# Layer statistics of two pairs on ScalarE, one scale on GpSimd, one block of zero matmuls out, and a new order of steps

## What is computed

```python
qf = jnp.fft.fft(q, axis=2)
kf = jnp.fft.fft(k, axis=2)
corr = jnp.fft.ifft(qf * jnp.conj(kf), axis=2).real
w, idx = jax.lax.top_k(corr.transpose(0, 1, 3, 2), topk)      # topk = 8
w = jax.nn.softmax(w, axis=-1)
out = sum over i of w_i * v[min(pos + idx_i, L - 1)]
...
x = x + jnp.tanh(g_xattn[0]) * xattn(_layernorm(x), ctx, ctx)
x = x + jnp.tanh(g_ffn[0]) * ffn(_layernorm(x), W_gate, W_up, W_down)   # (silu(gate) * up) @ W_down
```

## Time and profile before

| | us |
|---|---|
| median of 3 runs (213.5 to 214.62) | 214.24 |
| span of the profiled execution | 212.1 |
| TensorE busy in it | 203.6 |
| VectorE | 135.7 |
| ScalarE | 131.4 |
| GpSimd | 122.4 |

### The profile page before, as it was taken

How to read it: one execution, slowest core, us unless ns; L and a number is a source line. 1 busy time by engine, 2 the same in 40 slices (tenths; PEclk the granted TensorE clock), 3 DMA queues, 4 the chain that set the end, 5 groups by cost and what they waited for, 6 DMA issues and landing times.

```text
span 212.1 us, 6601 instructions
## 1 busy us (share of the span) xinstructions
PE 203.6 (96%) x2700; PEld 147.8 (70%) x2700; DVE 135.7 (64%) x408; ACT 131.4 (62%) x207; POOL 122.4 (58%) x151
## 2 busy tenths in 40 slices
PE   7889799999999999999999999999999999999993
PEld 2344369855398866795689665896598669859992
DVE  2499978977987884689478933898454426412411
ACT  2581776789897989697947894986335713502220
POOL 1200658588598977589848596797724734610430
PEclk9999999999999999999999999999999999999999
DMA  6999986420222201002011211120213300211001
GB/s 154 338 416 434 389 297 137 106 44 12 49 35 47 25 3 38 14 3 51 0 28 30 49 28 25 53 53 2 71 31 66 134 3 0 77 25 53 5 0 51
DMA packets 20734, 17.89 MB, mean 84 GB/s; under 512 B 16096, under 2 KB 16992, under 8 KB 20320
## 3 DMA queue, kind: packets, MB, share of 16 engines
q1 hardware_dynamic: 20704, 17.47, 27.5%
HBM read 10.65 MB, written 2.10 MB: 60 GB/s over the span
## 4 chain that ended last, share of the span: by engine, by line
PE 89%; DVE 5%; ACT 1%; DMA 1%; issue 1%; POOL 1%; DVEq 0%; POOLq 0%
PE psum L937 48%; PE psum L1121 23%; PE psum L920 6%; PE psum L1071 3%; PE psum L928 2%; PE psum L1056 2%; DMA x_sb<-x 1%; PE psum L1048 1%; PE psum L1014 1%; DVE top L792 1%; DVE probs L814 1%; DVE raw_stats L759 1%; PE psum L1016 1%; PE psum L1015 1%; DVE prod L782 1%
## 5 line engine op out<-in xcount | busy, mean ns | idle before, releaser
L937 PE MATMUL psum<-xt_hi,wu 128*128 128x128 f16 (+1 forms) x504 | 54.0, 213 | 0.0
L937 PE MATMUL psum<-xt_lo,wu 128*128 128x128 f16 (+1 forms) x504 | 54.0, 213 | 0.0
L937 PE MATMUL psum<-xt_hi,wg 128*128 128x128 f16 (+1 forms) x504 | 54.0, 213 | 0.0
L937 PE MATMUL psum<-xt_lo,wg 128*128 128x128 f16 (+1 forms) x504 | 53.9, 213 | 0.0
L632 POOL TENSOR_TENSOR hid_lo<-hid,hid_hi 128x512 f16<-128x512 f32 (+2 forms) x32 | 33.6, 1055 | 28.8 <-ACT hid_hi L750 28.7
L937 PEld LDWEIGHTS psum<-xt_hi,wg 128*128 128x128 f16 x504 | 44.8, 98 | 5.6 <-issue 5.0
L937 PEld LDWEIGHTS psum<-xt_hi,wu 128*128 128x128 f16 x504 | 45.0, 98 | 3.2 <-issue 2.4
L937 PEld LDWEIGHTS psum<-xt_lo,wu 128*128 128x128 f16 x504 | 45.1, 98 | 0.7
L937 PEld LDWEIGHTS psum<-xt_lo,wg 128*128 128x128 f16 x504 | 45.0, 98 | 0.6
L1121 PE MATMUL psum<-wd,hid_hi 128*128 128x512 f16 (+1 forms) x126 | 43.3, 356 | 0.0
L1121 PE MATMUL psum<-wd,hid_lo 128*128 128x512 f16 (+1 forms) x126 | 43.3, 355 | 0.0
(11 more groups left out here) (95 smaller groups left out, 340.9 us busy)
## 6 DMA issues: line engine op xcount, KB each, us to landing
wg<-w_gate SPq DMA_DIRECT2D x1, 1792.0 KB, 8.9
wu<-w_up SPq DMA_DIRECT2D x1, 1792.0 KB, 12.8
wd<-w_down SPq DMA_DIRECT2D x1, 1792.0 KB, 16.9
out<-x_sb SPq DMA_DIRECT2D x7, 256.0 KB, 2.3
...
ctx_sb<-ctx SPq DMA_DIRECT2D x1, 1024.0 KB, 18.6
...
```

What stands on the lines that cost most here:

```text
L937: last = nc.tensor.matmul(psum[:, bank, a * n:(a + 1) * n], w[:, k, m * P:(m + 1) * P], xt[:, e, k, tok], start=(k == 0 and part == 0), st ...
```

## The change

First statistics of pairs 1 and 2. The step `stats1` is gone for them. Instead ScalarE copies `x` with its accumulator on (`xsum`, the sum over 512 columns), GpSimd makes the negative mean (`negmean`), ScalarE squares `x` minus the mean with its accumulator on (`xsq`), and `rstd1` on GpSimd works from that sum of squares. `normed` takes the copies, which nobody reads. The scale of the second batch of pair 0 (`scale:0.1`) goes from VectorE to GpSimd. The second block of zero matmuls is left out, the first stays.

Further: the token buffers `xt_hi` and `xt_lo` are four instead of two; every step of `down` signals its end, and `h_hi` waits for the step that frees its part; `w_whole` lies in `v_turned`, so that the turn of pair 2 waits for `wspec:0.1`; the second half of the last store is issued from ScalarE's queue. The functions for groups of pairs do nothing new here, since every group has one pair. And the table `ORDER` is a new one as a whole.

```diff
-vcopy:1 mask:0 max:0.1 kcopy:1.1 scale:0 sub8:0.1 wt:0 stats1:2 exp8:0.1 w_hi:0 match:0.1 gates:0 wspec:0
+mask:0 kcopy:1 turn:1.3 scale:0 max:0.1 q_norm:1 wt:0 sub:0.1 w_hi:0 match:0.1 kcopy:1.1 wspec:0 sub8:0.1 xsum:2
...
-ON_VECTOR = (("scale", 0, 0), ("scale", 0, 1),)
+ON_VECTOR = (("scale", 0, 0),)
+SUMMED = (1, 2)
...
-    w_whole = sb("w_whole", [P, 2, D])
+    w_whole = v_turned[:, 0, :, :]
...
-                        if p >= 2:
-                            sp.wait_ge(up_done, STEPS * (p - 1))
+                        if p >= 4:
+                            sp.wait_ge(up_done, tokens_used(p))
...
+                if step == "negmean":
+                    pool.wait_ge(summed, SUMMED.index(p) + 1)
+                    nc.gpsimd.tensor_scalar(minus_mean[:, e:e + 1], x_sum[:, e:e + 1], -1 / D, None,
+                                            ALU.mult).then_inc(mean_ready, 1)
+                if step == "rstd1" and p in SUMMED:
+                    pool.wait_ge(squared, SUMMED.index(p) + 1)
+                    nc.gpsimd.tensor_scalar(var_eps[:, e:e + 1], square_sum[:, e:e + 1], 1 / D, EPS, ALU.mult,
+                                            ALU.add).then_inc(eps1, 1)
...
+                if step == "scale" and p == 0 and mine:
+                    to = twice(n)
+                    pool.wait_ge(inv_ready, nth("total", p, n))
+                    pool.wait_ge(masked, nth("mask", p, n))
+                    nc.gpsimd.tensor_tensor(to, lag_cols(expo, p, n).unsqueeze(2).broadcast_to(to.shape),
...
+                if step == "xsum":
+                    act.wait_ge(x_loaded[load_of(p)], 16)
+                    if p >= 2 and p - 2 in WHOLE_SPECTRA:
+                        act.wait_ge(q_spectra, p - 1)
+                    nc.scalar.activation(normed[:, e, :], x_sb[:, p, :], ACT.Copy,
+                                         accum_out=x_sum[:, e:e + 1]).then_inc(summed, 1)
+                if step == "xsq":
+                    act.wait_ge(mean_ready, SUMMED.index(p) + 1)
+                    nc.scalar.activation(normed[:, e, :], x_sb[:, p, :], ACT.Square, bias=minus_mean[:, e:e + 1],
+                                         accum_out=square_sum[:, e:e + 1]).then_inc(squared, 1)
...
-                        act.wait_ge(down_done, p - 1)
+                        act.wait_ge(down_step, hidden_free(p, n))
...
+                if step == "store_half":
+                    act.wait_ge(out_ready, PAIRS + 1)
+                    nc.scalar.dma_start(outv[:, p:p + 1, halves(p)[1]], x_sb[:, p:p + 1, halves(p)[1]])\
+                      .then_inc(half_stored, 16)
```

290 lines of the change are left out of this document (174 added, 116 removed).

## The result

The changed kernel took 215.97 us in the median of six executions (214.19 to 217.05), the kernel before 214.09 (213.5 to 214.62, six executions). The ratio is 1.0083, with a 95% interval of 1.0051 to 1.0115. The forecast was 213.3, and its range ended at 214.8.

What follows compares the result with a forecast made beforehand. TensorE, full from 28 to 208 us, was taken as the bound, leaving only prologue and end to gain. 0.8 us at the front plus 0.1 at the end, off 214.24, gave 213.3 us, range 212.4 to 214.8.

Steps and rivals of the forecast that it cites:

- The front: Prologue up to gate:0: w_hi:0 at 14.2, mix_prod:0 at 16.0, max:1 near 20.8, gate:0 earlier by 0.8 us.
- the order of `max:0.1` and `scale:0`: VectorE in the prologue: scale:0 ahead of max:0.1 takes 0.53 us off the path, 0.10 given back.
- the place of `scale:0.1`: VectorE from mix_prod:0 to max:1: scale:0.1 goes out, four small steps come in, net gain 0.18 us.
- the sum: Whole kernel: 0.8 us at the front plus 0.1 at the end, 0.9 us off the time.
- pair 2's statistics: Prologue: leaving VectorE gives nothing; on ScalarE two activations between 15.7 and 17.6 us, through before anyone waits.
- The accumulator: ScalarE, two more activations per pair: each at least 0.54 us, at most 0.80 plus 0.2 for reading the sum.
- The rival that put ScalarE late: Prologue: accumulators cost 0.6 us more than taken up to w_hi:0, giving 214.0 us; chance 0.17.
- `scale:0.1` on GpSimd: Prologue: 1.04 us on GpSimd, from near 19.3 to 20.4, hidden by 0.3 us behind lags:1.
- The end: Last stores: the second issued from ScalarE's queue instead of SyncE's, gain 0.1 us, bounds 0 and 0.2.
- The turns: SyncE's queue: eight DMAs of pairs 1 and 2 moved ahead of pair 1's first weight transposes, no cost.
- The clock: TensorE in the prologue, second zero block out: clock falls, 2.8 us more, 216.1 us; chance 0.10.
- New order opens holes: Full stretch, 28 to 208 us: holes of 0.69 us, one gives 214.0, three 215.4; chance 0.10.

Runs made afterwards that it cites:

- e9: Kernel before with max:0.1 behind scale:0 on VectorE, scale:0.1 on GpSimd behind lags:1 and the second store split off: 213.72 us beside 213.79, ratio 1.0002.
- e10: Changed kernel's order up to gate:0 with five zero matmuls, gates:0, k_hi:3, k_lo:3 and turns at their old places, old order behind: 213.71 us beside 213.79.
- e11: Kernel before with the statistics of pairs 1 and 2 on ScalarE's accumulator, each where its step stood, second store split off: 216.95 us beside 213.79, ratio 1.0104.
- e12: Kernel before with SyncE's turns of pairs 1 and 2 moved ahead, nothing else: 217.50 us beside 213.79, ratio 1.0132.
- e1: Changed kernel with five zero matmuls put back ahead of wt:0: 215.51 us beside 213.78, ratio 1.0064.
- e5: e1 with SyncE's turns of pairs 1 and 2 put back behind w_t:1 and w_t:1.1: 214.52 us beside 213.90, ratio 1.0023.
- e17: The changed kernel as it is, timed again beside the kernel before: 215.86 us beside 213.94, ratio 1.0083.
- e18: Changed kernel with only the turns put back behind w_t:1 and w_t:1.1, second zero block still out: 215.82 us beside 213.94, ratio 1.0029.
- e2: Kernel before without its second block of zero matmuls, nothing else changed: 215.26 us beside 213.78, ratio 1.0075.
- e6: Kernel before up to gate:0, the changed kernel's order from there on, turns where they stood: 214.91 us beside 213.90, ratio 1.0045.
- e13: e10 with a third block of four zero matmuls ahead of wspec:0.1: 213.41 us beside 213.91, ratio 0.9989.
- e16: e13 with the one 1 MB load of ctx moved to just ahead of w_t:2: 213.89 us beside 213.94, ratio 0.9984.

## Why the prediction was wrong, step by step

**The front: right.** `w_hi:0` was forecast at 14.2 and stands at 14.02, `mix_prod:0` at 16.0 and stands at 15.84, `max:1` at 20.8 and stands at 20.71. The gain at `gate:0` is 0.9 us where 0.8 was said. How it was shared out was less right: e9 shows that the order of `max:0.1` and `scale:0` and the place of `scale:0.1`, which carried 0.61 of the sum (0.53 - 0.10 + 0.18), give nothing while pair 2's statistics stay on VectorE. And a `gate:0` 0.9 us earlier is not 0.9 us off the time: TensorE then comes to instruction 450 before its block is ready. With the turns back and the old rest behind it (e10, at full clock 213.15 to 213.46) about 0.5 us is left.

**The accumulator: its duration right, its risk too small.** The two activations took 0.63 and 0.71 us and each reading 0.20, within the bounds given. That pair 2's statistics cost nothing held in the change's places; e11 shows 1.0% by its ratio and 3.2 us by the medians (216.95 - 213.79), lost clock included, for the work of both pairs at the places of the steps that it replaces. The rival that put ScalarE late, at 0.17, did not come in: `w_hi:0` started at 14.02.

**`scale:0.1` on GpSimd: right.** 1.04 us at 19.17, waited for by nobody; `wt:0.1` starts at 20.51.

**The end: right, a little more.** 0.23 us where 0.1 was taken and 0.2 was the bound.

**The turns: wrong, and the largest miss.** The prediction wrote of SyncE's turns moved ahead: "No cost." It asked who waits for SyncE, and nobody did. It did not ask what eight transfers of 128 KB do to the DMA queues, which are full until about 30 us (DMA share 1.06 in 28 to 30 us of the kernel before, 0.48 in 30 to 32), and what else goes through them: TensorE's own instructions, whose second block of the stretch came 1.8 us later in e12. Measured: 1.3% alone (e12), 1.0 us in the change (e1 against e5), 0.7 us at full clock (e17 against e18). The last two are net of the wait for `w_t:1.1` that putting them back brings.

**The clock: a rival at 0.10 that came in.** Its price was taken at 2.8 us between 1.39 and 4.5. Alone the missing block costs 1.5 us (e2), and it came in in 4 of 6 and 8 of 12 executions of the change. The mechanism was named rightly; what was wrong is the chance. The sum itself removed the last work in a TensorE idle of 1.41 us and then called the full clock the likely case, with only the kernel before, which had the block, to show it.

**New order opens holes: a rival at 0.10 that came in.** One hole was priced at 214.0, three at 215.4. Measured: 1.0 us alone (e6), 0.75 in the change's profile, of which 0.53 is `out:2` behind `sub8:5`.

**Put together**, for the profiled execution: 0.9 off at the front, 0.65 back in 28 to 40 us, 0.75 back in 60 to 120 us, 0.2 off at the end, which gives +0.3 us of span, as measured. The medians lie 1.9 us apart (215.97 and 214.09), so the typical execution lost 1.6 us more than the profiled one; the lower clock and longer gaps in 28 to 40 us (e17's profile, at full clock, has 1.6 us of them) are there to carry it, but no profile of the change at the lower clock divides it between them. Three things that had a small chance, or none, came together. Each is a cost alone (e12, e2, e6), though their prices do not add up.

No version here beats the kernel before beyond doubt. The nearest are e13 (0.9989, 0.9966 to 1.0011) and e16 (0.9984, 0.9949 to 1.0019).
